# Cross-attention and expert FFN on one core: 24 shared tiles ahead of the routed units and 8 behind, low weight parts spread, and PSUM operands behind the units

## What is computed

```python
x = x + xattn(layernorm(x), ctx)
def expert(x, w1, b1, w3, b3, w2, b2):
    h = silu((x @ w1 + b1) * (x @ w3 + b3))
    return h @ w2 + b2                      # D = 256, H = 352
y = sum over the 2 chosen experts e of score_e * expert(x, w1[e], ...)
z = expert(x, sw1, sb1, sw3, sb3, sw2, sb2) # shared
x = x + y + z                               # x on the right normalized for y and z
```

## Time and profile before

| | us |
|---|---|
| median of 3 runs | 726.75 |
| lowest and highest | 723.37, 728.51 |
| the profiled execution | 728.36 |
| its span in the trace | 726.6 |
| PE busy in the span | 670.8 (92%) |
| DVE busy | 537.5 (74%) |
| POOL busy | 429.4 (59%) |
| ACT busy | 401.2 (55%) |

### The profile page before, as it was taken

One profiled execution on the slowest core, in us unless ns is written; L12 is line 12 of the kernel. 1 busy time (PEld: TensorE's weight loads), 2 busy tenths in 40 slices (PEclk: granted clock), 3 DMA queues, 4 the chain that ended last, 5 costly groups with the idle time before them and its releaser, 6 DMA issues.

```text
span 726.6 us, 16827 instructions
## 1 busy us (share of the span) xinstructions
PE 670.8 (92%) x4614; PEld 627.2 (86%) x4615; DVE 537.5 (74%) x1106; ACT 401.2 (55%) x1308; POOL 429.4 (59%) x514
## 2 busy tenths in 40 slices
PE   7996789999999999984799999999999999999976
PEld 6785679998888889874698999999999999999975
DVE  6966588888978888757889766666666666666696
ACT  5975577877767768745544444444444444444432
POOL 4544465454468768665444346677777777775391
PEclk9989899999999999997999999999999999999999
DMA  8301223336526886546731334454444444455594
GB/s 243 82 15 51 80 74 97 100 115 188 164 78 122 201 136 121 138 103 127 126 75 41 82 50 72 74 74 72 72 73 72 72 72 72 72 102 101 146 405 190
DMA packets 77046, 79.03 MB, mean 109 GB/s; under 512 B 21739, under 2 KB 70229, under 8 KB 76981
## 3 DMA queue, kind: packets, MB, share of 16 engines
q1 hardware_dynamic: 56932, 53.66, 28.9%
q0 software_dynamic: 15760, 18.96, 16.0%
q10 hardware_dynamic: 4288, 5.64, 2.3%
HBM read 47.22 MB, written 31.01 MB: 108 GB/s over the span
## 4 chain that ended last, share of the span: by engine, by line
PE 67%; DVE 11%; issue 9%; POOL 5%; ACT 4%; DMA 3%; SPq 0%; DVEq 0%; ACTq 0%; POOLq 0%
PE ps L1289 56%; PE ps L1480 4%; PE ps L1351 3%; PE ps L1472 2%; PE ps L1335 1%; DVE uv L1215 1%; DMA xin<-in_x 1%; DVE hTl L1202 1%; DVE AU L1141 1%; POOL xrow L726 1%; DVE w13l L1173 1%; PE ps L1320 1%; DMA wk_raw<-in_L_xattn_Wk 1%; DMA acc_scratch<-yrow,slots 1%; ACT AU L818 1%
## 5 line engine op out<-in xcount | busy, mean ns | idle before, releaser
L733 POOL DMA_INDIRECT acc_scratch<-yrow,slots x71 | 112.7, 1588 | 75.3 <-ACT yrow L938 57.2
L938 ACT ACTIVATE yrow<-ps,slots 128x256 f32<-128x256 f32 x71 | 33.8, 475 | 147.5 <-PE ps L1289 147.5
L1289 PE MATMUL ps<-AU,pTh 128*128 128x256 f32 x512 | 101.6, 290 | 0.0
L1215 DVE TENSOR_TENSOR uv<-ps,b 128x704 f32<-128x704 f32 x71 | 63.3, 891 | 47.8 <-PE ps L1289 47.8
L1289 PE MATMUL ps<-w13h,uxTh 128*128 x284 | 97.7, 344 | 0.0
L1289 PE MATMUL ps<-AU,xTh 128*128 128x512 f32 x256 | 95.4, 417 | 0.0
L1289 PE MATMUL ps<-w13h,uxTl 128*128 x284 | 91.6, 322 | 0.0
L1289 PE MATMUL ps<-w13l,uxTh 128*128 x284 | 91.3, 322 | 0.0
L676 POOL DMA_INDIRECT slots_scratch<-record,slot x64 | 65.7, 1027 | 42.5 <-DMA slots_scratch<-record,slot 29.3
L726 POOL DMA_INDIRECT xrow<-xn_scratch,slots x71 | 69.8, 984 | 27.2 <-issue 19.8
L1289 PEld LDWEIGHTS ps<-AU,pTh 128*128 128x128 f32 x512 | 82.6, 192 | 0.0
(11 more groups left out here) (241 smaller groups left out, 2002.1 us busy)
## 6 DMA issues: line engine op xcount, KB each, us to landing
sums<-acc_scratch SPq DMA_DIRECT2D x16, 512.0 KB, 11.5
w_raw<-in_L_ffn_w SPq DMA_DIRECT2D x16, 352.0 KB, 4.2
xin<-in_x SPq DMA_DIRECT2D x32, 128.0 KB, 2.6
xres<-in_x SPq DMA_DIRECT2D x32, 128.0 KB, 3.0
acc_scratch<-x SPq DMA_DIRECT2D x32, 128.0 KB, 2.1
xn_scratch<-xn SPq DMA_DIRECT2D x32, 128.0 KB, 2.6
xn2T_scratch<-xn2T SPq DMA_DIRECT2D x32, 128.0 KB
xrow<-xn2T_scratch SPq DMA_DIRECT2D x32, 128.0 KB, 2.4
```

Source lines behind the costliest of these rows:

```text
L733: pool.indirect_dma_start(acc_dram[u % 2], bass.IndirectOffsetOnAxis(ap=slots[:, u, 0:1], axis=0), yrow[:, m % YRING, :], None, compute_op ...
L938: act.activation(yrow[:, y, :], ps[:, 6 + m % 2, 0:D], ACT.Copy, scale=slots[:, bass.ds(u, 1), 1].bitcast(F32)).then_inc(y_ok, 1)
L1215: dve.tensor_tensor(uv[:, :, :], ps[:, 1 + 2 * p:3 + 2 * p, 0:H], bias, ALU.add).then_inc(bias_ok, 1)
L1289: last = pe.matmul(out, stationary(k, a), moving(k, b), start=(k == 0 and i == 0), stop=(k == n - 1 and i == len(PARTS) - 1 and not more))
```

## The change

NA goes from 20 to 24 and NB from 12 to 8. Routed units are now 24 to 94, the tiles behind 95 to 102. The low weight parts are made in other steps: `low13` of experts 3 to 7 in steps 4, 8, 12, 16 and 20, `low2` of experts 0 to 7 in steps 6, 10, 14, 18, 22, 24, 25 and 26. PE waits for them in two parts. For the tiles behind, ACT writes the input row a second time, into PSUM, and DVE reads it there; the bias add is split into two instructions, of which the second writes its half (v) back into PSUM, where the product reads it. The 16 bias loads become 2.

```diff
-    NA = 20
+    NA = 24
-        b13 = sb("b13", [P, E, 2 * H], F32)
+        b13 = sb("b13", [P, 2, E, H], F32)
+        LOW13 = (4, 8, 12, 16, 20)
+        LOW2 = (6, 10, 14, 18, 22, 24, 25, 26)
+        LOW13_READY = 3 + len(LOW13) + len([i for i in LOW2 if i < LOW13[-1]])
@@ SP
-            for e in range(E):
-                for i, b in enumerate((b1, b3)):
-                    sp.dma_start(b13[:, e, i * H:(i + 1) * H],
-                                 b[e, :].rearrange("(a h) -> a h", a=1).to_broadcast([P, H])).then_inc(b13_in, 16)
+            for i, b in enumerate((b1, b3)):
+                sp.dma_start(b13[:, i, :, :].rearrange("p e h -> p (e h)"),
+                             b.rearrange("(a e) h -> a (e h)", a=1).to_broadcast([P, E * H])).then_inc(b13_in, 16)
@@ ACT, unit_step
-                    act.activation(uxTh[:, p, :], xT, ACT.Copy).then_inc(uxTh_ok, 1)
+                    if isinstance(t, int) and t >= R1:
+                        act.wait_ge(uxTl_ok, R1)
+                        act.activation(uxTh[:, p, :], xT, ACT.Copy)
+                        act.activation(ps[:, 0, p * D:(p + 1) * D], xT, ACT.Copy).then_inc(uxTh_ok, 1)
+                    else:
+                        act.activation(uxTh[:, p, :], xT, ACT.Copy).then_inc(uxTh_ok, 1)
@@ DVE, unit_step
-                    xT = ps[:, 0, 0:D] if is_routed(t, routed) else xrow[:, m, :]
+                    if is_routed(t, routed):
+                        xT = ps[:, 0, 0:D]
+                    elif t >= R1:
+                        xT = ps[:, 0, p * D:(p + 1) * D]
+                    else:
+                        xT = xrow[:, m, :]
-                    dve.tensor_tensor(uv[:, :, :], ps[:, 1 + 2 * p:3 + 2 * p, 0:H], bias, ALU.add).then_inc(bias_ok, 1)
+                    raw_u, raw_v = (ps[:, 1 + 2 * p + i, 0:H] for i in range(2))
+                    if isinstance(t, int) and t >= R1:
+                        dve.tensor_tensor(uv[:, 0, :], raw_u, bias[:, 0, :], ALU.add)
+                        dve.tensor_tensor(raw_v, raw_v, bias[:, 1, :], ALU.add).then_inc(bias_ok, 1)
+                        v = raw_v
+                    else:
+                        dve.tensor_tensor(uv[:, :, :], ps[:, 1 + 2 * p:3 + 2 * p, 0:H], bias, ALU.add).then_inc(bias_ok, 1)
+                        v = uv[:, 1, :]
-                    dve.tensor_tensor(hid[:, p, 0:H], uv[:, 0, :], uv[:, 1, :], ALU.mult).then_inc(z_ok, 1)
-                if isinstance(s, int) and 5 <= s < 5 + E:
-                    low2(s - 5)
-                if isinstance(s, int) and 5 + E <= s < 5 + E + E - 3:
-                    low13(s - 5 - E + 3)
+                    dve.tensor_tensor(hid[:, p, 0:H], v, uv[:, 0, :], ALU.mult).then_inc(z_ok, 1)
+                if isinstance(s, int) and s in LOW13:
+                    low13(3 + LOW13.index(s))
+                if isinstance(s, int) and s in LOW2:
+                    low2(LOW2.index(s))
@@ PE, unit_step
-                        pe.wait_ge(w_lo, 2 * E)
+                        pe.wait_ge(w_lo, LOW13_READY)
+                    if isinstance(t, int) and t == R0:
+                        pe.wait_ge(w_lo, 2 * E)
-                    wait(pe, bias_ok, t - 1)
+                    wait(pe, z_ok if isinstance(t, int) and t >= R1 + 2 else bias_ok, t - 1)
```

More of the change, by code:

```diff
@@ L384, in xattn_moe @@
         LAG = 4
+        LOW13 = (4, 8, 12, 16, 20)
+        LOW2 = (6, 10, 14, 18, 22, 24, 25, 26)
+        LOW13_READY = 3 + len(LOW13) + len([i for i in LOW2 if i < LOW13[-1]])
+        assert NA <= LOW2[-1] < R0 + LAG - 1
         FILL = 5
@@ L1208, in unit_step @@
                         if isinstance(t, int) and t == R0:
-                            dve.wait_ge(b13_in, 32 * E)
-                        bias = b13[:, bass.ds(e, 1), :].rearrange("p e (a h) -> p (e a) h", a=2)
+                            dve.wait_ge(b13_in, 32)
+                        bias = b13[:, :, bass.ds(e, 1), :].rearrange("p a e h -> p a (e h)")
                     else:
```

## The result

The changed kernel is slower: a median of 742.67 us (736.01 to 745.32, 6 runs) against 724.95 us (721.72 to 728.51, 6 runs) of the kernel before beside it. The ratio is 1.0229, with a 95% interval of 1.0194 to 1.0264, that is +16.6 us; the medians themselves are 17.7 apart. The forecast was 739.8, in a range of 734 to 744: the sign and the range held, the size came out 2.9 us short.

The account below looks back on a forecast made before the run. PE bounds 465 to 678 us; changes count only where PE waits, chiefly the tail's eight adds. Terms +8.88 +0.2 +0.2 +1.67 +0.6 -1.0 +2.5 = +13.05 on 726.6: span 739.65, median 739.8, range 734 to 744.

Parts of the forecast that it names:

- The adds gate step 103: Tail: DVE's first result add waits for all eight group adds; 13.31 us later start minus 4.43 us slack, +8.88 us.
- the slack of 4.43 us: Tail of the kernel before: DVE reaches the first result add 4.43 us after the last group add ends.
- PSUM operands: Tiles behind the units: `uxTl` and `hid` keep their time beside POOL, but the gain is hidden by the wait; 0.
- The rival that they don't escape: Steps 99 to 102 stay slowed at 5.1 us each, total still 739.8 us; no chance of its own given.
- ACT's second copy: Steps 95 to 98: the copy delays `hTl` by 0.3 to 0.4 us against slack; +0.2 us, between 0 and 0.5.
- Low parts: Front: `low13` in step 4 costs +1.67 us, four lone ones instead of five in a row cost +0.6.
- Gather waits: Routed units: PE's waits for later gathers shrink as the units start later; -1.0 us, between -2.1 and 0.
- The clock at the end: From step 104: PE restarts at the lower clock after some 14 us idle; +2.5 us, between 0 and +3.3.
- the third rival: Front: the clock falls there too, one or two more steps run low, +1.6 to +3.2 us, 742.2 us; chance 0.17.

Follow-up runs that it names:

- first trace: The changed kernel without further edit, profiled execution of its first measurement: 736.01 us, the shortest of its six runs.
- The move alone: The kernel before with NA = 24 and nothing else changed: 739.0 us against 729.2, ratio 1.0144.
- chip 10: The changed kernel without further edit, measured and traced a second time, against the kernel before: 745.95 us against 729.2, ratio 1.0247.
- chip 5: The changed kernel without further edit, measured and traced a third time, against the kernel before: 743.89 us against 731.21, ratio 1.0162.
- PE kept busy at the end: The changed kernel with 120 transposes of the identity added on PE ahead of Y of unit 100: 744.94 us, ratio 1.0175 to the kernel before.

## Why the prediction was nearly right

Point by point, in the order of its sum, against the first trace:

- *The adds gate step 103 (+8.88).* Shown. DVE waited 15.01 us (13 to 17 were named); the adds' end lies 32.4 us after the last routed Y (32.61); the slack of 4.43 us was used up to 0.03. With the adds reordered the wait is gone. The adds took 2.40 us beside DVE and 2.34 once DVE was idle. The move alone measured +9.8 for 10.4.
- *PSUM operands (0 here).* Shown. `uxTl` 0.43, `hid` 0.53, no slowing beside POOL. The gain is hidden behind the wait here, and it is 3.7 us in the trace where nothing waits. The rival that they don't escape fell.
- *ACT's second copy (+0.2).* Mis-sized. The four steps up to the last routed Y took 14.47 us for 13.54. That is +0.9, above the 0 to 0.5 that was named, and it delays the start of the chain of the adds in full. Steps 99 to 102 took 3.40 us for 3.33 as well, but those lie in front of the wait.
- *Low parts (+2.3).* Right against a step at the upper clock, and not against the trace that the sum started from. Its arithmetic held: `low13` in step 4 gave 6.95 - 5.39 = +1.56 for 1.67, a lone `low13` 4.11 - 3.33 = +0.78 for 0.80. Against the move alone, at clock 1.00 in both, the three steps from step 4 on took 15.73 for 14.07 us, +1.66. What failed is a reason: the `low2` leaving step 5 "gives nothing back, since in the next step PE runs at clock 0.52". It gives nothing back indeed (3.42 us with it and 3.43 without, at clock 1.00), but the lower clock there was not a fixed property of that step. It was a cost of 1.6 us that one execution of the kernel before had. Step 6 in it, and the same in the move alone:

```profile
358.38 0.38 PE L1289 MATMUL ps<-ws2h,hTh 128*128 128x256 f32 x1 [1.80 <-DVE hTl L1202]
...
363.37 0.29 PE L1289 MATMUL ps<-ws2h,hTh 128*128 128x256 f32 x1
...
358.39 0.39 PE L1289 MATMUL ps<-ws2h,hTh 128*128 128x256 f32 x1 [1.71 <-DVE hTl L1202]
...
361.81 0.28 PE L1289 MATMUL ps<-ws2h,hTh 128*128 128x256 f32 x1
```

  In the first trace the clock stayed up, the distance was 3.43, and that hid the `low13`: 5.35 + 6.95 + 3.43 = 15.73 us for the three steps, as much as the 5.35 + 5.39 + 4.99 of before. In the second it fell, and for longer, 6.03, and the three steps took 18.3. So they came out between 0 and +2.6 us against the one trace of before.
- *Gather waits (-1.0).* Right by one measure and too large by another. In the table of waits PE's waits for gathers are 0.3 us in all after and were 1.3 before (the profile's page has 2.1 for them). But the time from Y of the first routed unit to Y of the 68th, 243.0 us before, is 242.5, 243.0 and 242.8 in the three traces of the changed kernel, and 241.6 with the move alone. Why the changed kernel gains less than the move alone is open. The first routed transposes are at 420.58; from the last gate matmul that is 93.7 us after and 79.3 before, 14.5 more, for 15.3 forecast.
- *The clock at the end (+2.5).* Right in place and mechanism, and a range rather than a number: 2.0, 2.95 and 0.7 us in the three traces. The busy shares of 69% and 71% by which it was argued did not decide it: the clock was at 0.68 in step 5 of one execution and at 1.00 in that of another with the same steps (the table in the section before).

The Trainium skill (TensorE: Matmul & The Clock Gate, part 1) has the chip judge PE's activity on a schedule of its own, which does not start with the kernel, so that the same kernel may come out differently. The two equal idles with different clocks (3.36 and 3.32 us) agree with it. The Trainium skill (SBUF — State Buffer, Who interferes with whom) has a VectorE instruction with two SBUF inputs contend with a GpSimd instruction that reads SBUF, for a port pair that one of them holds alone. The rows agree, 2.51 and 0.43 us for the same subtraction.

By the medians the excess over the sum is 17.7 - 13.05 = 4.7 us in the first measurement, 3.7 on chip 10 and -0.4 on chip 5. ACT's second copy is 0.7 of it, each time. The traces show two larger things, each in some executions: the clock fall in front (2.6 us in the second trace), which was the third rival with a chance of 0.17 at 742.2 us. That the median came out at 742.67 does not bear this rival out, as two of the three traces don't have the fall. The other is the late input tile (up to 4.8 us), which was in no rival. The lower mean clock of the four longer timed runs (0.955 to 0.965 for 0.971 and 0.973) fits falls of the clock, without saying where they were. How the excess divides between the two stays open. The sum was made against one profiled execution, low clock in front included, and its difference to the median, 1.6 us, was carried over as if both kernels spread alike. That the first trace of the changed kernel came within 0.6 us of the sum (12.5 for 13.05) is in part luck: the 1.6 us of clock that it did not lose in step 6 hid as much of the `low13`.

## What to carry to other kernels

Work placed behind the last user of a buffer or a result may be there as cover for a chain of transfers and sums that starts when that user ends. Before moving it, compare the chain's length with what remains: the adds need 32.6 us, the twelve tiles behind brought step 103 at 37.0 us (33.3 once undisturbed), and with eight tiles it would have come 13.3 earlier. When an engine's instruction is slow only beside another engine, change one of its operands to the other memory first, and look at whether the time it wins lies on the path: the same edit gave 3.7 us in the tail of one arrangement and nothing in the other, and the extra copy that it needs cost 0.9 us in both. Whether that cost can be saved by starting the copy only where the slow instructions are was not tried. And a lower clock seen in one execution is not a fixed price: give it a range from both levels, and ask which engine sets the pace in the step where it falls.

## What the runs showed of the hardware that was not expected

- The granted clock after a given idle of PE is not fixed. After 3.3 us of idle it was 0.52 for a whole step in one execution and 1.00 in another of the same kernel; after 13.6 to 14.4 us of idle it stayed low for three Y's, two, or one. In steps 5 and 6 it fell in eight of fourteen traces, also where PE had not been idle for more than 1.8 us at a time in the 15 us before. In the second profile of the PSUM operands alone the last two Y's ran low after idles of only 2.02 and 1.47 us.
- A DVE instruction with one PSUM and one SBUF operand keeps its time beside a POOL add (0.43 and 0.53 us), while one with two SBUF operands takes 2.39 for 1.22 (1024 elements) and 2.51 for 0.42 (256 elements). That would fit a wait for the end of POOL's 2.4 us instruction better than a share of its speed; it was not tested.
- The attention stage of one kernel ended anywhere from 326.8 to 336.8 us in three executions; waits of 0.96 to 4.08 us for one input tile are a part of it.
- In five executions (PE kept busy at the end, and in front; low13 from step 7; PSUM and adds reordered; the PSUM operands alone, again) DVE or ACT stood still for 1.5 to 4.1 us between 407 and 421 us, and the trace gives the releaser only as remote. In the changed kernel's own three traces the steps there are even. Its cause is open.
